# Attention of a two-block vision model: the running order of the row maxima, of the first transfers and of the projection weights

## The reference, cut to what matters

```
q, k, v = split(x @ qkv_w.T + qkv_b)              # 4 images, 12 heads, 1024 tokens, 16 wide
bias    = rel_h(q)[..., :, None] + rel_w(q)[..., None, :]   # not in the third attention
attn    = softmax(q @ k.T * scale + bias)         # 1024 x 1024 per head
out     = (attn @ v) @ proj_w.T + proj_b
```

## Time and profile before

| | |
|---|---|
| median of three executions | 3696.29 us (3686.05 to 3705.49) |
| the profiled execution, its own time | 3690.02 us |
| its span, first to last instruction | 3688.4 us |
| TensorE matmul busy | 3147.2 us (85%) |
| VectorE busy | 2612.5 us (71%) |
| ScalarE busy | 1978.5 us (54%) |
| GpSimd busy | 280.7 us (8%) |
| bytes moved by DMA | 252.02 MB, 68 GB/s over the span |
| mean granted TensorE clock | 0.903 |

### The profile page before, as it was taken

One profiled execution on the slowest core, in us unless ns is written; L12 is line 12 of the kernel. 1 busy time (PEld: TensorE's weight loads), 2 busy tenths in 40 slices (PEclk: granted clock), 3 DMA queues, 4 the chain that ended last, 5 costly groups with the idle time before them and its releaser, 6 DMA issues. The chain is left out here.

```text
span 3688.4 us, 66977 instructions
## 1 busy us (share of the span) xinstructions
PE 3147.2 (85%) x20624; PEld 1427.2 (39%) x20624; DVE 2612.5 (71%) x5066; ACT 1978.5 (54%) x2643; POOL 280.7 (8%) x371
## 2 busy tenths in 40 slices
PE   5939999987999999693999998438999996869998
PEld 3602222233666666461222223212222234636676
DVE  6359999966666666545999996649999964556655
ACT  4317777755333333431776775426777764555555
POOL 0010111110000000001011111010111110000000
PEclk8659999997999999775999999668999997889999
DMA  2465676632000000047576773020111110020000
GB/s 67 159 134 107 135 140 139 135 81 83 13 0 0 0 0 0 25 162 137 103 139 132 143 139 82 16 81 27 48 45 52 51 41 17 0 65 9 9 4 13
DMA packets 179970, 252.02 MB, mean 68 GB/s; under 512 B 50974, under 2 KB 73646, under 8 KB 179850
## 3 DMA queue, kind: packets, MB, share of 16 engines
q1 hardware_dynamic: 147962, 201.06, 25.0%
q10 hardware_dynamic: 18784, 31.87, 2.7%
q0 software_dynamic: 13104, 17.60, 2.3%
HBM read 182.80 MB, written 66.65 MB: 68 GB/s over the span
## 5 line engine op out<-in xcount | busy, mean ns | idle before, releaser
L750 DVE TENSOR_REDUCE c1att_mx<-c1att_m 128x1 f32<-128x512 f32 x768 | 493.8, 686 | 64.5 <-PE c1att_m L688 58.9
L750 DVE TENSOR_REDUCE c0att_mx<-c0att_m 128x1 f32<-128x512 f32 x768 | 494.1, 686 | 62.8 <-PE c0att_m L688 57.9
L750 DVE TENSOR_REDUCE f1att_mx<-f1att_m 128x1 f32<-128x512 f32 x768 | 493.7, 685 | 25.0 <-PE f1att_m L688 20.5
L989 ACT ACTIVATE c1att_p<-c1att_s 128x1024 f32<-128x1024 f32 x384 | 372.1, 1021 | 154.8 <-PE c1att_s L703 154.5
L989 ACT ACTIVATE c0att_p<-c0att_s 128x1024 f32<-128x1024 f32 x384 | 372.1, 1021 | 149.3 <-PE c0att_s L703 148.9
L989 ACT ACTIVATE f1att_p<-f1att_s 128x1024 f32<-128x1024 f32 x384 | 372.1, 1021 | 118.5 <-PE f1att_s L703 117.5
L1408 ACT ACTIVATE f_s<-f_u 128x512 f32<-128x512 f32 x192 | 114.7, 597 | 373.4 <-PE f_u L1333 373.4
L1497 DVE SCALAR_TENSOR_TENSOR f_h<-f_u,f_s 128x512 f32<-128x512 f32 x192 | 132.7, 691 | 149.4 <-ACT f_s L1408 145.5
L1416 ACT ACTIVATE moe_h<-moe_u,moe_bu 128x512 f32<-128x512 f32 x192 | 136.7, 712 | 175.5 <-PE moe_u L1333 93.7
L688 PE MATMUL f1att_m<-f1att_km,f1att_qm 16*128 16x512 f16 x768 | 154.6, 399 | 71.8 <-DVE f1att_ka L952 52.8
L716 PE MATMUL c0att_o<-c0att_p,c0att_vs 128*32 128x512 f32 x1536 | 210.4, 621 | 0.6 <-ACT c0att_p L989 0.6
(11 more groups left out here) (561 smaller groups left out, 5974.5 us busy)
## 6 DMA issues: line engine op xcount, KB each, us to landing
xt<-rel_parts SPq DMA_DIRECT2D x256, 128.0 KB, 6.3
xt<-qk_parts SPq DMA_DIRECT2D x192, 128.0 KB, 5.0
y<-rel_parts SPq DMA_DIRECT2D x128, 128.0 KB, 5.3
y<-qk_parts SPq DMA_DIRECT2D x96, 128.0 KB, 4.7
c0att_qm<-rel_parts SPq DMA_DIRECT2D x144, 64.0 KB, 2.2
c1att_qm<-rel_parts SPq DMA_DIRECT2D x144, 64.0 KB, 2.2
o_sums<-c0att_o ACTq DMA_DIRECT2D x24, 256.0 KB, 2.5
o_sums<-c1att_o ACTq DMA_DIRECT2D x24, 256.0 KB, 2.4
```

The lines of the kernel that those rows point to most:

```text
L750: dve.tensor_reduce(mx[:, n:n + 1], bank[:, :], AX.X, ALU.max).then_inc(s_mx, 1)
L989: act.activation(pr[h][kt % 2][:, :], sps[h][:, :], ACT.Exp).then_inc(s_e, 1)
```

## The change

The change has five edits, all in `attention`:

1. EARLY goes from 14 to 22. START then holds 22 maxima of pair 1, and a pair's steps hold (1, 22) to (1, 31) and (2, 0) to (2, 21). The last product of the next pair moves from step 5 to the first slot of step 3.
2. The row moves from the end of step 5 to behind the scores of step 4, ahead of (2, 2) and (2, 3). ROWS is 3, so ScalarE copies it after the exponentials numbered 3.
3. In START the row of pair 0 comes behind the first two maxima of pair 1.
4. SyncE's queue places the row of pair 0 ahead of the loads of pairs 1 and 2, but behind the maxima operands of pair 1.
5. The projection weights and bias are issued by ScalarE's queue.

```
-        EARLY = 14
-        ROWS = 5
+        EARLY = 22
+        ROWS = 3
         items, PLAN = [(1, n) for n in range(EARLY, MAXES)] + [(2, n) for n in range(EARLY)], []
         for step in range(1, KT + 1):
             PLAN.append([[items.pop(0) for _ in range(2)] for _ in range(2)])
-            if step == ROWS:
-                PLAN[-1][1] += [(1, "row")]
+            if step == ROWS + 1:
+                PLAN[-1][0].insert(0, (1, "row"))
...
-        START = [(0, n) for n in range(MAXES)] + [(0, "row")] + [(1, n) for n in range(EARLY)]
+        START = [(0, n) for n in range(MAXES)] + [(1, 0), (1, 1), (0, "row")] + [(1, n) for n in range(2, EARLY)]
...
             def _(sp):
-                for j in range(2):
-                    sp.dma_start(pw[:, j * C:(j + 1) * C], wo[j * HALF:(j + 1) * HALF, :]).then_inc(s_pw, 16)
-                sp.dma_start(bias[:, :], bo.broadcast_to([P, C])).then_inc(s_pw, 16)
-                for u in range(RING):
+                def first_maxima(u):
+
                     for h in range(2 if rel else 0):
                         sp.dma_start(km[u][64 * h + HD:64 * h + 64, :], spots).then_inc(s_lm[u], 16)
                     load_maxima(sp, u, u)
+
+                def first_load(u):
+
                     for h in range(2 if rel else 0):
                         sp.dma_start(ka[u][R_REL:R_QK, h * L:(h + 1) * L], hot).then_inc(s_ld[u], 16)
                     load(sp, u, u)
...
+                first_maxima(0)
+                first_load(0)
+                first_maxima(1)
                 place_rows(sp, 0, 0)
+                first_load(1)
+                first_maxima(2)
+                first_load(2)
                 load_maxima(sp, RING, 0)
                 place_rows(sp, 1, 1)
...
+                for j in range(2):
+                    act.dma_start(pw[:, j * C:(j + 1) * C], wo[j * HALF:(j + 1) * HALF, :]).then_inc(s_pw, 16)
+                act.dma_start(bias[:, :], bo.broadcast_to([P, C])).then_inc(s_pw, 16)
                 act.wait_ge(s_pw, 3 * 16)
                 act.activation(pwh[:, :], pw[:, :], ACT.Identity, scale=W_SCALE).then_inc(s_pwh, 1)
                 act_row(act, 0, 0, mps[START.index((0, "row")) % 3])
```

## The result

On one chip, four executions of each kernel: 3633.39 us after (3630.71 to 3637.59) against 3698.29 before (3686.05 to 3705.49), a ratio of 0.983 with an interval of 0.980 to 0.986. The profiled execution took 3630.71 us, 59.3 under that of before (3690.02). Forecast was 3636. In the rounds of the experiments the medians of before were 3689.6 to 3692.6, so that 3698.29 lies high and the gain is nearer to 59 than to 65 us.

A forecast was written before the change was run, and what follows sets the result against it. It took TensorE and VectorE to be in balance in the loop, 21.67 us a pair, plus row waits. c0att -28.2, c1att -29.1 and f1att +3.5 sum to -53.8 us, from 3690.0 to 3636 us; range 3602 to 3678.

The forecast's parts named there:

- The loop's waits, -21.3 and -19.4: Loops of c0att and c1att: with more room all waits for row DMAs go, saving 21.3 and 19.4 us.
- f1att is a control: f1att's loop, with far smaller loads, loses 5.1 us, mostly to seven reciprocals; what c0att and c1att lose beyond it is the bias's.
- The waits before: c0att's loop before: seven TensorE waits for row DMAs, 13.9 us, against 21.3 us lost, a factor of 1.5.
- A landing stays where it is against the copy: Loop: SyncE's chain moves with the row, so the latest landing, 8.05 us, fits into the room of 9.7 us.
- the waits stay: Rival, loop: landing moves out as far as the row moves in, the 40.7 us stay; 3677 us, chance 0.16.
- The starts: Before the first scores: 9.0 us sooner in c0att, 10.8 in c1att and 1.0 there by edit 5; 5.4 later in f1att.
- The row of pair 1, +4: Pair 0 of c0att and c1att: this row lands late, a 2.7 us wait that costs 4 us each.
- The undisturbed pair, 0: Loop: the bank rule still holds (2, 2) until (2, 1) is reduced, so the pair stays at 21.67 us; gain 0.
- the idle goes too: Rival, loop: VectorE's 0.48 us idle a pair goes as well, 32 us more gain; 3604 us, chance 0.14.
- The end, -1.9: End of each attention: two fewer steps with maxima save 1.0 us, TensorE's wait for the last negative about 0.9.
- f1att, +3.5: f1att as a whole: 5.4 us later from eight uncovered products, less 1.9 at the end.
- Maxima operands in the loop as the slower rival: Rival, step 3 of some 44 pairs: maxima operands land late and TensorE waits; w = 1.5 gives 3735 us, chance 0.05.

The follow-up runs named there:

- the starts alone: Edits 3, 4 and 5 alone on the kernel of before, 14 ahead and the row at the end of step 5: 3684.7 us, ratio 0.998.
- the second one with split sums: The kernel with split weighted sums, but in f1att alone 14 maxima ahead and the row behind step 6's scores: 3659.96 us against 3661.95.
- 18 ahead: The changed kernel with 18 products ahead instead of 22 and the row behind step 5's scores: 3657.12 us, ratio 0.992.
- the experiment with the earlier reciprocal: The kernel with 18 products ahead, with VectorE's reciprocal 8 reductions earlier so that GpSimd's transfer goes out sooner: 3647.32 us, ratio 0.989.
- The early row: The changed kernel, with SyncE issuing maxima operands of pair 2 ahead of load 1, pair 1's row and pair 3's maxima operands ahead of load 2: 3615.58 us.
- The run with the banks apart: The changed kernel, but products (2, 2) and (2, 3) each wait for their own bank alone: 3633.48 us, ratio 0.985.
- Leaving out the row's place: The kernel with pair 1's row early, without the row's product in the loop or its place in the ring of banks: 3578.5 us.
- both together: The changed kernel with pair 1's row issued early and the banks apart: 3616.84 us.
- the first split: On the kernel with pair 1's row early and the banks apart, half of step 4's weighted sums moved between (2, 2) and (2, 3): 3661.95 us.
- the two that leave work out: The kernel with pair 1's row early, without the row's product in the loop: 3618.48 us; without its place in the ring too: 3578.5 us.

## Why the prediction was right, point by point

The mechanism was right: the row's waits in the loop went with the longer room, a new wait came for the row of pair 1, and the undisturbed pair stayed. The sum was right partly by luck: the loops gave some 11 us more than forecast, the starts 1.5 and f1att's first pair 1.1 more, while the late row of pair 1 with the maxima operands cost 8 more and the ends gave 2.7 less.

- **The loop's waits, -21.3 and -19.4.** Mis-sized. Less the long distance's excess of 6.5 to 6.7, the 22 distances shrank by 25.0 and 22.2 us, and f1att's by 4.1, for which 0 stood. The step that failed is "f1att is a control" with 5.1 us of loss that stays, "mostly the seven reciprocals": after the change, with the same reciprocals, the three lose 1.4, 2.3 and 1.0 us over 22 x 21.67. Part of f1att's loss before was four negatives that took 0.36 to 1.04 us beside a GpSimd operation, instead of 0.17; the distances that end with them are 3.1 us over 4 x 21.67. The two other kernels with 14 ahead in f1att (the starts alone, and the second one with split sums) have five and four such negatives there; no kernel with the row in step 4 has one there. The longest before:

```profile
2738.58 1.04 DVE L759 TENSOR_SCALAR f1att_m<-f1att_m 128x16 f16<-128x16 f32 x1
```

- **The waits before.** The seven waits of 13.9 us left out an eighth, of 1.20 us at 758.55, which the profile puts down to another operand (`xt<-rel_parts`). That operand's semaphore was full at 758.05 and the row's at 758.47, so this too was a wait for the row. With it the waits are 15.1 us and the factor on them 1.4, not 1.5.
- **"A landing stays where it is against the copy."** True of the kernel with 22 ahead, but not for the reason given, that SyncE's chain moves with the row: with 18 ahead the latest landing is 9.3 and 9.6 us behind the copy. With 22 it is 7.3, which leaves 2.4 us of the room of 9.7; the latest with 18, 9.6, would have been at its edge. The chance of 0.16 for "the waits stay" named the phase against GpSimd, rightly, and the experiment with the earlier reciprocal shows it as a cause. That the phase fell well with 22 was not worked out beforehand.
- **The starts.** First scores: -9.0 was forecast in c0att and -10.3 came, the difference being edit 5, which was costed at 0 there: VectorE's operation on the weights took 0.79 us instead of 2.05 (they began at 204.59 and 204.72). Before, it began 0.17 us behind a GpSimd operation of 1.81 us, and after the change 1.42 us behind it; with the weights back on SyncE it is 0.15 behind and takes 2.06. In c1att -11.8 and -12.1, in f1att +5.4 and +5.5.
- **The row of pair 1, +4.** Mis-sized. It was issued at 265.47 (265.4 forecast), but the scores could begin only 8.1 us later, at 273.5 and not 271: a wait of 5.0, not 2.7. The maxima operands, costed at 0 because 255 was before 256.9, were wanted at 255.5 and came at 257.2, a wait of 1.77 (1.22 in c1att); such a wait was named as a sign of being wrong, and it appeared, though in pair 0 alone. The early row shows the price of both, 8.6 and 8.1 us in the two stages, a factor of 1.3 on the waits where 1.5 was used.
- **The undisturbed pair, 0.** Right, and so was the bank as its reason. The run with the banks apart seemed to refute it; its edit left (2, 3) tied to (2, 1). Leaving out the row's place settled it. The 32 us of "the idle goes too" are there, but not by changing what one couple waits for: the row must give up its bank.
- **The end, -1.9.** It was -1.0 in each stage: from the last copy to the last weighted sums 21.5 us became 25.3; with the row's earlier place, 4.8, and the forecast's -1.9 it would be 24.4. The wait of 0.90 us for the last negative is gone as forecast. TensorE waits for ScalarE's exponentials there now (0.40 us at 744.69, 0.30 at 745.59).
- **f1att, +3.5.** It was -0.7: the loop's -4.1 came instead of 0, the end gave 0.9 less, and 1.1 us went in its first pair. The last is small luck: in the five other kernels that give f1att the same plan and compute everything with whole sums, its last weighted sums come at 568.8 to 570.2 us, so the change is -0.7 to +0.8.
- **Maxima operands in the loop as the slower rival.** No wait for them came behind pair 0, as forecast.

## What to carry to other kernels

Where a small transfer comes late, look at its place in the queue first: taking the row of pair 1 and two sets of maxima operands each ahead of one load was worth 17 us in the two stages, while 16 us of earlier first scores without it kept 2 (c0att, the starts alone). Never take one stage as a control without reading its own stalls. When a chain on one queue is moved, look at where it falls against the other queue's transfers. Before costing an edit to one wait, write down every user of the buffer (here the third bank) until the ring has turned.

## What the runs showed of the hardware

In these traces VectorE's negative, a small operation from SBUF to SBUF, does not end before a GpSimd operation that it begins beside. With 18 ahead, in f1att, VectorE's timeline and then GpSimd's:

```profile
2762.36 2.32 DVE L759 TENSOR_SCALAR f1att_m<-f1att_m 128x16 f16<-128x16 f32 x1
```

```profile
2762.32 2.33 POOL L924 TENSOR_TENSOR f1att_t<-f1att_t 96x1024 f32<-96x1024 f32 x1 [5.29 <-DMA f1att_t<-rz_rows]
```

It began 0.04 us after GpSimd's and ended 0.03 after it, 2.32 us in place of 0.17, and the pair took 23.6 us. In nine of these runs (all but the weights back on SyncE, both together, the first split and the two that leave work out) 36 negatives begin inside a tensor_tensor or cast of GpSimd; each ends 0.03 to 0.11 us after it. The 1534 reductions from PSUM that begin inside such operations all took 0.67 to 0.69 us. The Trainium skill, "SBUF — State Buffer", "Who interferes with whom", says that the two engines' shared ports are an exclusive lock, taken by whichever begins first and only by some operations of VectorE, not by a reduction; this trace agrees.

The weighted sums write four groups of 32 output partitions; in the kernel with split sums all four take 1.00 us from start to start (411.38 to 412.38), and two of them 0.99 (414.20 to 415.19). By the Trainium skill, "TensorEngine Tiling (Array Packing)", "Key Properties", different tiles of the array run in parallel; the trace agrees. Splitting such a group cost this kernel 45 us.
